# A fused attention-and-experts block: 36 expert steps for 39, eight of them with two experts on two column halves

## The reference

```python
x = x + quantised_two_layer_block(layernorm(x), fside, ctx)      # per batch, int8-like rounding
t = layernorm(x)
w, idx = top_k(softmax(t @ router_w), 2);  w = w / sum(w)
for e in the two experts of a row:                                # gate, up: 512 -> 256; down: 256 -> 512
    x = x + w[e] * ((silu(t @ gate[e]) * (t @ up[e])) @ down[e])
```

## Time and profile before

| what | us |
|---|---|
| median of 3 runs | 382.58 (381.6 to 385.44) |
| the profiled execution, its own time | 381.06 |
| its span, first to last instruction | 379.3 |
| TensorE busy | 321.9 (85%) |
| GpSimd busy | 244.5 (64%) |
| VectorE busy | 225.1 (59%) |
| ScalarE busy | 202.9 (54%) |

### The profile page before, as it was taken

One profiled execution on the slowest core, in us unless ns is written; L12 is line 12 of the kernel. 1 busy time (PEld: TensorE's weight loads), 2 busy tenths in 40 slices (PEclk: granted clock), 3 DMA queues, 4 the chain that ended last, 5 costly groups with the idle time before them and its releaser, 6 DMA issues.

```text
span 379.3 us, 6450 instructions
## 1 busy us (share of the span) xinstructions
PE 321.9 (85%) x1955; PEld 189.8 (50%) x1955; DVE 225.1 (59%) x515; ACT 202.9 (54%) x382; POOL 244.5 (64%) x271
## 2 busy tenths in 40 slices
PE   4698757877798885679899899999999999999980
PEld 1455435545665652375574455555555555555530
DVE  3588887879899988878678732333333333333320
ACT  1557568888897796139635234444444444444430
POOL 6486697879999971685461472656667746675441
PEclk9999999999999999999999999999999999999997
DMA  7765446745765508147127554557687657786544
GB/s 247 245 264 196 136 163 199 265 147 165 277 258 188 189 35 242 64 167 232 75 31 275 86 144 80 101 99 116 129 137 115 125 95 123 132 137 107 92 55 55
DMA packets 27551, 56.79 MB, mean 150 GB/s; under 512 B 2624, under 2 KB 13888, under 8 KB 25600
## 3 DMA queue, kind: packets, MB, share of 16 engines
q0 software_dynamic: 8736, 20.45, 29.9%
q1 hardware_dynamic: 17968, 35.39, 27.0%
q10 hardware_dynamic: 816, 0.54, 0.5%
HBM read 37.50 MB, written 18.87 MB: 149 GB/s over the span
## 4 chain that ended last, share of the span: by engine, by line
PE 33%; POOL 22%; issue 17%; DVE 14%; ACT 5%; DMA 4%; POOLq 2%; SPq 0%; DVEq 0%; ACTq 0%
PE bank_h L1328 13%; PE bank_q L1349 6%; POOL x L648 4%; POOL w_in L666 3%; POOL out L687 3%; DVE amax L726 3%; PE bank_t L1313 3%; PE bank_q L1194 2%; POOL w_in L619 2%; POOL gu_lo L584 2%; DVE rmax L756 2%; POOLq L682 2%; PE bank_h L1222 2%; ACT xn L1014 2%; DMA stage<-tokens,gather_at 2%
## 5 line engine op out<-in xcount | busy, mean ns | idle before, releaser
L1328 PE MATMUL bank_h<-gu_hi,xT 128*128 x312 | 103.9, 379 | 0.0
L1328 PE MATMUL bank_h<-gu_lo,xT 128*128 x156 | 59.1, 379 | 0.0
L970 DVE SCALAR_TENSOR_TENSOR xT<-bank_t,xT 128x512 f16<-128x512 f32 x39 | 26.8, 689 | 53.9 <-ACT xT L1104 53.8
L1349 PE MATMUL bank_q<-dn_hi,aT 128*128 x156 | 52.6, 379 | 1.7 <-DVE aT L988 1.4
L1328 PEld LDWEIGHTS bank_h<-gu_hi,xT 128*128 128x128 f16 x312 | 30.5, 98 | 29.3 <-issue 0.2
L666 POOL DMA_INDIRECT w_in<-tokens,gather_at x30 | 29.8, 993 | 17.8 <-issue 7.6
L584 POOL TENSOR_TENSOR gu_lo<-stage,gu_hi 128x1024 bf16<-128x1024 f32 x16 | 34.0, 2135 | 7.5 <-ACT gu_hi L1061 7.3
L978 DVE SCALAR_TENSOR_TENSOR gated<-bank_h,gated 128x256 f32<-128x256 f32 x39 | 16.5, 422 | 32.0 <-ACT gated L1111 32.0
L1111 ACT ACTIVATE gated<-bank_h 128x256 f32<-128x256 f32 x39 | 14.9, 383 | 38.0 <-PE bank_h L1328 38.0
L726 DVE TENSOR_REDUCE amax<-bank_t 128x1 f32<-128x512 f32 x48 | 30.8, 684 | 6.6 <-PE bank_t L1194 4.7
L687 POOL DMA_INDIRECT out<-h,scatter_at x17 | 26.9, 1580 | 11.8 <-DMA out<-h,scatter_at 4.5
(11 more groups left out here) (197 smaller groups left out, 704.5 us busy)
## 6 DMA issues: line engine op xcount, KB each, us to landing
stage<-in_L_ffn_gate_proj SPq DMA_DIRECT2D x8, 512.0 KB, 4.2
stage<-in_L_ffn_up_proj SPq DMA_DIRECT2D x8, 512.0 KB, 4.1
stage<-in_L_ffn_down_proj SPq DMA_DIRECT2D x8, 512.0 KB, 4.9
x<-in_x SPq DMA_DIRECT2D x4, 1024.0 KB, 6.3
out<-x SPq DMA_DIRECT2D x4, 1024.0 KB, 4.6
tokens<-xn SPq DMA_DIRECT2D x4, 1024.0 KB, 4.5
x_in<-in_x SPq DMA_DIRECT2D x3, 1024.0 KB, 7.5
w_in<-in_fside_BxS2xS SPq DMA_DIRECT2D x3, 1024.0 KB, 5.6
```

The source lines that it names most:

```text
L970: dve.scalar_tensor_tensor(out=xT[i % 2][:, 1].rearrange("p c t -> p (c t)"), in0=bank, scalar=X_SCALE, in1=xT[i % 2][:, 0].rearrange("p c ...
L1328: ins = pe.matmul(bank, xT[i % 2][:, part, c], rhs[:, cols], start=(c == 0 and m == 0), stop=(c == C - 1 and m == 2))
L1349: ins = pe.matmul(bank, aT[i % 2][:, part, c], rhs[:, cols], start=(c == 0 and n == 0), stop=(c == FC - 1 and n == 2))
```

## The change

There are 28 whole tiles (`WHOLE`) and 8 mixed ones (`MIXED`), 36 in all. Expert e's rows are cut into halves of 64. Its whole tiles hold 128 rows; what is left, under 128 rows, goes to mixed tile e: the last, partial half into slots 64 to 127 and, where there is an odd full half, that into slots 0 to 63. Where an expert has more whole tiles than there is room for, they are cut in two, and each half goes to slots 0 to 63 of a mixed tile whose own expert leaves them free (the overflow rows). Mixed tiles are steps 15 to 22 (`MIXED_FROM` = 15), whole late tiles are steps 9 to 14 and 23 to 35.

In a mixed step each matmul becomes two of 64 columns, one to PSUM partitions 0 to 63 with the expert read from the register, one to 64 to 127 with the weights of expert i - 15 written in. Every mixed tile is added by two DMAs: `scatter` for the expert's own rows (128 slots, in which the overflow ones are sent to spare rows) and `scatter over` for slots 0 to 63. `landed` now counts these units one by one. The mixed tile's own scatter waits for the own scatter of the mixed tile before, and for its `scatter over` too if that holds overflow rows; a `scatter over` with overflow rows waits for the own scatter of its tile. The first whole tile behind (step 23) waits for all of them. GpSimd's late order is written out in `POOL_ORDER`, and the loop that made it is gone. VectorE gets four new stages ("halves", "mixed list", "mixed indices", "mixed turns"), TensorE one ("mixed indices"). `onesb`, `nothing` and `share` shrink to one column that is read 128 times.

```diff
@@ GpSimd's order, cut to its core
-    "residual 3, deviation 2 3, scatter 0, gather 6, gather 7, gap 2, scatter 1, gather 8, scatter 2, gather 9, "
-    "scatter 3, scatter 4, scatter 5, scatter 6, scatter 7, scatter 8")
+    "residual 3, deviation 2 3, scatter 0, gather 6, gather 7, gap 2, scatter 1, gather 8, scatter 2, "
+    "gather 9, gather 10, gather 11, scatter 3, gather 12, scatter 4, gather 13, scatter 5, gather 14, scatter 6, "
...
+    "gather 20, scatter 12, gather 21, scatter 13, gather 22, scatter 14, gather 23, scatter 15, scatter over 15, "
+    "scatter 16, scatter over 16, scatter 17, scatter over 17, gather 24, scatter 18, scatter over 18, gather 25, "
...
@@ block_kernel
-    TILES = (N * TOPK + E * (P - 1)) // P
+    MIXED = E
+    WHOLE = (N * TOPK // HALF - MIXED) // 2
+    TILES = WHOLE + MIXED
+    UNITS = TILES - EARLY + MIXED
+    FULL = WHOLE - EARLY
+    AHEAD = MIXED_FROM - EARLY
@@ SyncE
-            for i in range(EARLY, TILES):
-                n = i - EARLY
-                sp.wait_ge(sem(f"added{n % (2 * J)}"), 16 * (n // (2 * J) + 1))
+            for n in range(UNITS):
+                sp.wait_ge(sem(f"added{n % (4 * J)}"), 16 * (n // (4 * J) + 1))
                 sp.sem_inc(sem("landed"), 1)
@@ scatter
+                elif i == MIXED_FROM:
+                    pool.wait_ge(sem("landed"), 1 + AHEAD)
+                else:
+                    k = i - MIXED_FROM
+                    before = pool.value_load(own_after[0:1, k - 1:k], min_val=1, max_val=1 + UNITS)
+                    pool.wait_ge(sem("landed"), before)
+                    hold(pool, i)
...
+            def scatter_over(i):
+                k = i - MIXED_FROM
+                before = pool.value_load(spill_after[0:1, k:k + 1], min_val=1, max_val=1 + UNITS)
+                pool.wait_ge(sem("landed"), before)
+                hold(pool, k)
+                add_rows(i, 1, y(i)[0:HALF], mixed_at[0:HALF, 0, k:k + 1])
@@ mixed_turns (VectorE); expert_number is k, flag is 1 where tile k holds overflow rows
+                then(dve.tensor_scalar(flag, free_at[:], spilled[:], None, ALU.is_lt))
+                then(dve.scalar_tensor_tensor(out=turn, in0=expert_number[:], scalar=2.0, in1=flag, op0=ALU.mult, op1=ALU.add))
+                dve.tensor_scalar(own_after[:], turn, AHEAD + 2.0, None, ALU.add).then_inc(sem("turns"), 1)
+                dve.scalar_tensor_tensor(out=spill_after[:], in0=turn, scalar=float(AHEAD), in1=flag, op0=ALU.add,
+                                         op1=ALU.add).then_inc(sem("turns"), 1)
@@ indices (VectorE), for the whole tiles behind the mixed ones
+                    then(dve.tensor_scalar(scatter_after[:, MIXED_END:TILES], sorted_out[:, 4, MIXED_END:TILES], float(AHEAD),
+                                           1.0 + 2 * MIXED, ALU.max, ALU.add))
@@ take_y (ScalarE)
-                        act.wait_ge(sem("landed"), before - EARLY + 2)
+                        act.wait_ge(sem("landed"), units_upto(before))
@@ gate_up (TensorE); down likewise
+                        if phase_of[i] < 2:
+                            ins = pe.matmul(bank, xT[i % 2][:, part, c], rhs[:, cols], start=start, stop=stop)
+                        else:
+                            pe.matmul(bank[0:HALF], xT[i % 2][:, part, c, 0:HALF], rhs[:, cols], start=start, stop=stop)
+                            own = (gu_hi, gu_lo, gu_hi)[m][:, i - MIXED_FROM, c]
+                            ins = pe.matmul(bank[HALF:P], xT[i % 2][:, part, c, HALF:P], own, start=start, stop=stop)
```

More of the change, by code:

```diff
@@ new lines, in mark_halves @@
+            def mark_halves(_):
+                last, odd, even = (ending[:, n:n + 1] for n in range(3))
+                own = owners[:, 1]
+                then(dve.tensor_tensor(last, slot_row[:], owned_sum[:, 2:3], ALU.is_equal))
+                then(dve.tensor_tensor(odd, last, owned_sum[:, 3:4], ALU.mult))
+                then(dve.tensor_tensor(even, last, odd, ALU.subtract))
+                then(dve.tensor_scalar(own_onehot[:, 0], own, even, None, ALU.mult))
+                then(dve.tensor_scalar(own_onehot[:, 1], own, odd, None, ALU.mult))
+                for half in range(2):
+                    then(dve.tensor_scalar(spill_onehot[:, half], free_at[:], low_at[:, half:half + 1], beyond[:], ALU.is_equal, ALU.mult))
+                dve.tensor_tensor(low_onehot[:], spill_onehot[:, 0], own_onehot[:, 1], ALU.add).then_inc(sem("halves_listed"), 1)
@@ L1261, in rank @@
                     pe.wait_ge(sem("base_ready"), g)
[L1262 removed]
+                pe.matmul(rank, share[:].to_broadcast([P, P]), spread(base[g][:], [P, m + 1, E], 1), start=True, stop=False)
                 pe.wait_ge(sem("mask_ready"), g + 1)
```

180 lines of the change are left out of this document (134 added, 46 removed), and 5 rows, old and new, of tables (DVE_ORDER, PE_ORDER, POOL_ORDER).

## The result

The changed kernel takes 401.13 us (median of 4 runs, 400.35 to 402.66) beside 382.88 for the kernel before (4 runs, 381.60 to 385.44). The ratio is 1.048, with a 95% interval of 1.044 to 1.052: slower by 18 us. The profiled execution took 400.38 us, with a span of 398.6.

What follows compares the result with a forecast made beforehand. TensorE's pace bounds the kernel before; after, GpSimd's chain of scatters waiting for landings does. Scatter 35 at 386.6 plus 8.3 us of tail is 394.9, plus 1.8 beyond the span 396.7, put at 396.5 us; range 388 to 405.

Steps and rivals of the forecast that it cites:

- Three steps for 13.8 us: TensorE's late steps: three of 39 steps, on empty tiles, go at 4.60 us each, 13.8 us less of TensorE.
- TensorE no longer sets the end: Against the rival (0.05) that TensorE keeps the end, faster: 375 us, or 367 with both added terms hidden.
- 0.6 us a mixed step: TensorE, eight mixed steps: four turns between 64 and 128 columns cost 0.6 us a step, 5 us in all.
- the rival of halves that don't overlap: Rival, 0.07: in mixed steps the two column halves run one after the other, 3.9 us more a step; 407 us.
- VectorE's 12 small instructions cost 2.5 to 3.5 us at step 11: VectorE between a low 9 and x low 11: TensorE waits 2.5 to 3.5 us at step 11, not reaching the end.
- The chain: GpSimd's late scatters from scatter 3 at 221.5 to 35 at 386.6; 18 waits through SyncE's count (rounds), 5.5 us each.
- Rounds weren't short (4.95): Rival, 0.07: GpSimd's waits through SyncE's count take 4.95 us when little is in flight; 386 us, no difference.
- The counts were those of the router: Rival: other expert counts by the kernel's rounding, no overflow rows, two rounds less, 386 us; counted under no difference.
- Halves of rounds by the page's rule: GpSimd's 64-row transfers: a fixed 2.0 us plus the bytes, so half the rows would save 0.3 us of a round.
- What would show it: Signs: TensorE's share below 80%, some 17 `hold` waits of 2.5 us, scatter over 15 5.5 us behind 15, steps 4.6 to 5.4.
- The clock in TensorE's waits: Rival, 0.12: TensorE's clock falls while it waits for gathers; step 34 takes up to 4.6 us more, 401 us.
- The median of the runs is 1.5 us above the profiled one, and I leave it so.: Whole kernel before: the median's 1.5 us above the profiled execution, within the runs' spread, was not added to the forecast.

Runs made afterwards that it cites:

- the run with filler matmuls: Changed kernel with 8 to 18 unneeded matmuls ahead of TensorE's waits for gathers 24, 25, 26, 30, 32 and 35: 397.29 us, ratio 1.038.
- the run with all eight flags: Changed kernel with gathers 18 to 35 drawn forward, and the flag for overflow rows set to 1 for all eight mixed tiles: 408.07 us, ratio 1.063.
- that of 0.984: Changed kernel, gathers 18 to 35 drawn forward, mixed tiles' scatters to spare rows without waits among themselves, mixed steps' matmuls at full width: 377.67 us, ratio 0.984.
- The two orders: Changed kernel with GpSimd's gathers drawn forward: from gather 9 on, 384.54 us, ratio 1.003; only gathers 18 to 35, 385.06 us, ratio 1.004.
- the run without waits: Changed kernel with gathers 18 to 35 drawn forward and the mixed tiles' 16 scatters to spare rows, without waits among themselves: 379.92 us, ratio 0.991.

## Why the prediction was right, point by point

The forecast was 396.5 us in a range of 388 to 405, slower with a chance of 0.88. It came to 401.13, slower, by the mechanism named: rounds on GpSimd, gathers behind them, TensorE waiting from step 23 on. (The waits were for gathers 24, 25, 30, 32 and 35; the prediction had 26 for 24.)

- **Three steps for 13.8 us**: 14.4 measured by themselves.
- **TensorE no longer sets the end.** Right in the main: with the mixed steps' extra gone, 2 us of 4.3 came back (between nothing and 5).
- **0.6 us a mixed step.** Takes are 5.08 us apart for 4.54, so 0.54. The halves overlap fully, though each streams its own weights; the pairs start together, 0.215 us from the next pair:

```profile
262.27 0.38 PE L1476 MATMUL bank_h<-gu_hi,xT 128*64 x1
262.28 0.38 PE L1478 MATMUL bank_h<-gu_hi,xT 128*64 128x512 f16 x1
262.49 0.38 PE L1476 MATMUL bank_h<-gu_hi,xT 128*64 x1
262.49 0.38 PE L1478 MATMUL bank_h<-gu_hi,xT 128*64 128x512 f16 x1
```

  That settles the rival of halves that don't overlap. By the Trainium skill (TensorEngine Tiling (Array Packing), "Key Properties") a change of mode drains TensorE; 0.54 us for a step's four changes agrees.
- **VectorE's 12 small instructions cost 2.5 to 3.5 us at step 11.** From the take of tile 3 to that of tile 9 it is 242.98 - 217.21 = 25.8 us for the 238.04 - 215.40 = 22.6 of before: 3.1 us, and hidden at the end, as said.
- **The chain.** Scatter over 15 was forecast at 284.6 and came at 287.8; scatter 19 at 311.1 and 311.86; 23 at 335.9 and 336.52; 30 at 367.7 and 367.61; gather 35 at 369.6 and 369.47. The whole chain is right to 0.2 us at its end, but that is luck in part, by errors that cancel. It began 2.65 us late (224.15 for 221.5). Two of the three rounds behind 64-row transfers took 4.20 and 4.19 us (287.80 to 292.00, 307.67 to 311.86) for my 5.0, the third 5.69 (330.83 to 336.52). Why the third was long no run shows; the run with filler matmuls had 4.30 there. The full rounds within the mixed tiles took 4.9 to 5.4 for my 5.5.
- **The other rivals.** Rounds weren't short (4.95): the full ones took 5.1 to 5.8 us in the changed kernel, but for a single one of 4.93. The counts were those of the router: scatters over 15 and over 18 waited, 5.4 and 4.9 us behind their scatters, the other six stood 1.9 to 3.3 behind.
- **Halves of rounds by the page's rule.** In the prediction the Trainium skill (DMA: Bandwidth & Descriptors, "Anatomy of one DMA"), a fixed part plus the bytes, gave 0.3 us for half the rows. From scatter 15's start to the next `hold` it is 5.04 us, from scatter over 15's start 3.86: 1.2 us less; for tile 18 it is 4.59 and 3.85. In the run with all eight flags it is 4.57 to 6.26 behind the eight of 128 rows and 3.54 to 3.96 behind the eight of 64. Only over 22 falls out, with 5.35. The measurement decides: where the 64-row addition was waited for directly, half the rows saved more than the 0.3 us.
- **What would show it.** `hold` waits for the count 15 times for 17, 2.4 us each; over 15 starts 5.4 us behind 15; mixed steps of 5.1 us. Scatter 15 to 23 took 54.1 us for 56.8. TensorE's share is 83%, not below 80%: busy time grows at half the clock, so a share of busy time was the wrong sign to name, and the 14.5 us of waits for gathers the right one.

Where the 4.6 us missing lie, along the profiled execution: gather 35 was on time, y(33) came 3.1 us late and scatter 35 3.2 (389.79 for 386.6), the tail behind it was 0.5 longer (8.8 for 8.3), and so the execution took 400.38 us for the 396.7 of the sum. The median lies another 0.75 above it, and the forecast was put 0.2 below its sum. Two terms that the prediction had in view and put at nothing bear on this:

1. *The clock in TensorE's waits*, the rival with 0.12. I priced it at up to 4.6 us on step 34 and left it out of the forecast. It was there: y(33) was ready at 382.2 for the forecast 379.1, and against the run with filler matmuls the step costs 2.9 us more, less than 4.6 since the clock is back within the step. Forecast and rival weren't alternatives; what was left to ask was only whether waits of 2 to 5 us are long enough, and four of the five were.
2. *"The median of the runs is 1.5 us above the profiled one, and I leave it so."* The profiled execution of before, 381.06 us, lay below all three timed ones. The part that neither kernel changes took longer in that of after, with the same instructions and a lower clock. The columns are those of the earlier trace rows; first before, then after:

```profile
140.00:160.00 20.00, 12.45 (x84) 7.02 (x82) 17.51 (x51) 9.68 (x22) 8.02 (x6) 1.00 0.44 134
```

```profile
140.00:160.00 20.00, 13.73 (x80) 7.44 (x78) 16.41 (x50) 9.73 (x22) 6.45 (x5) 0.83 0.42 131
```

   The take of tile 3 comes 1.8 us later. Such dips of the clock stand somewhere in part one in the profiles of all other runs, of the kernel before with 36 tiles too (4.3 us later there, at 219.67), so the profile of before was the odd one. These 1.8 us are most of the 2.65 by which the chain began late, and the short rounds made them up before gather 35. So they are no part of the 4.6, of which only the 0.75 belongs here. A forecast of a median should still have started from the median.

**The ledger**, from ratios to the kernel before (1% is 3.83 us): three steps less, -14.4; the mixed tiles with no gather in the way, +16.0 (from 0.963 to 1.004); the gathers behind rounds, +16.8 (from 1.004 to 1.048), of which the clock is about 3. Sum +18.4. Of the 16.0, 4.9 are waits among the mixed tiles as such (to 0.991) and 2 to 3 TensorE's mixed steps (to 0.984), with intervals that touch. No run takes the other 8 away, but two traces tell where they lie, that of 36 plain steps and that of 0.984. From the take of tile 3 to that of tile 35 it is 140.1 and 142.2 us, so TensorE has 2 of them; scatter 35 starts 1.0 and 7.5 us behind the take of its rows, so GpSimd's lateness has the other 6 to 7: eight more transfers in its queue, and then the rounds from scatter 23 on.

No version here that does the whole computation for any inputs beats the kernel before. The two orders come level with it; what remains, 18 rounds in place of 7, follows from giving each expert a mixed tile of its own, and neither order takes it away. Whether fewer, fuller mixed tiles or additions of two experts in one transfer would do, wasn't tried.

## What to carry to other kernels

Before cutting work on the busiest engine, count what the new cut adds to serial chains elsewhere: here 14 us of TensorE were bought with eleven more waits for a landing, at 4 to 5 us each, on a queue that was already four steps behind. An in-order queue that carries both the waits at the end of the pipeline and the loads at its head turns every added wait into a late load; draw the loads forward by as many stages as the queue lags. Lay other work of the queue into such waits, but only as much as fits, since it lies bare when the wait gets shorter.

## What the runs showed of the hardware

- A 64-row accumulating scatter (2 KB a row) takes 1.43 to 1.5 us of GpSimd for its descriptors, against 1.55 to 1.6 for 128 rows. From its start to the `hold` behind its count it took 3.54 to 3.96 us in the run with all eight flags, against 4.57 to 6.26 for 128 rows. Half the rows saved a quarter of a round and next to nothing of the queue; one 64-row scatter of the changed kernel took 5.35.
- An addition with its value load and `hold` takes 1.86 to 1.97 us of GpSimd's queue and a gather 1.3. Two additions and a gather took 5.13 us in the run without waits, as much as TensorE's mixed step of 5.08.
- Two matmuls of 64 columns on the two halves of the array, with different weights and different accumulators in one bank, cost what one of 128 columns costs: 0.215 us. The four changes between 64 and 128 columns in a step cost 0.54 us together.
- Behind four idle times of 2.51 to 4.54 us within otherwise full work the granted clock fell, to 0.51 to 0.72 in the stretches that follow; behind one of 1.64 us it stayed at 1.00. The step behind the last of them took 2.9 us more for it. Unneeded matmuls in these waits kept the clock at 1.00 in the two stretches shown and won back 2.3 of the 2.9 us.
